# A mixture-of-experts layer behind gated linear attention: the joined passage, smaller padding, and expert numbers loaded one slot ahead

## The chip, the cores and the metric

The kernel runs on one core of a Trainium2 chip. The metric is the device time of one execution in microseconds; lower is better. The core has five engines with queues of their own: TensorE (PE in the profile, its weight loads PEld), VectorE (DVE), ScalarE (ACT), GpSimd (POOL) and SyncE (SP), which here only issues DMAs. Each engine works through its instructions in the order in which the program lists them, and semaphores order the engines against each other.

## The reference

The input is 2048 tokens of 128 channels in float32. First comes gated linear attention with 4 heads: each head carries a state through the tokens, `S = S * exp(g) + k v^T`, and the output `q S` is normalised by its RMS, gated, and projected; the layer's input is added, and a layer norm gives `x1`. Then comes the expert part:

```python
scores = x1 @ Wr + br                       # 8 experts
topk_idx = top_k(scores, 2)                 # 2 experts for each token
weights = softmax(scores over the 2 chosen)
for i in range(8):
    h = relu(x1 @ W1[i] + b1[i])            # 512 hidden
    y = h @ W2[i] + b2[i]
    out += y * weight of expert i           # for the tokens that chose i
x = layernorm(x1 + out)
```

## The kernel before, in words

The attention runs over T = 16 tiles of 128 tokens in ROUNDS = 20 software-pipelined rounds, written out by hand on every engine: in round i, tile i is scored, tile i-1 is attended (`AGE_O`), tile i-2 gets its gate (`AGE_GATE`), tile i-3 its projection, residual, layer norm and router score (`AGE_OUT`), and each pair of tiles its places among the experts' rows (`AGE_PLACE`). Two PSUM banks are handed over as wholes once in a round: PE writes bank 6 for ScalarE (`write_act_bank`) and bank 7 for VectorE (`write_dve_bank`), and it writes a bank again when the last reader is through.

The chosen rows of tokens (x1, the weight, and the number of the result row, 130 words) are scattered by POOL to a table in DRAM, `expert_rows`, in which each of the 8 experts has a region of CAP = 2176 rows (`scatter_rows`, L512 to L516; two indirect DMAs for a tile). The regions are not full, so SP first writes padding rows over all of them (L408 to L410, 8 DMAs of 1105 KB); POOL waits for the padding before the first scatter (L532).

The expert part works in SLOTS = 39 slots of 128 rows. A slot belongs to one expert; a small table in SBUF gives for every slot the expert and the first row. It is worked out on the core in two halves. The first EARLY = 13 slots follow from the first 10 tiles alone (`early_counts`, `early_pairs`, `early_positions`, `early_slots`, `early_entries`, `early_table`, a chain that alternates between PE and VectorE, begun in round EARLY_ROUND = 16); the other 26 from all tiles (`late_pairs`, `late_positions`, `late_slots`, `late_entries`, `late_table`, inside the first slots). The last of these early steps stand in round 17: PE's `early_entries` ahead of its `write_dve_bank(17)`, VectorE's `early_table` at the start of the round.

For each slot, SP reads the first row from the table and gathers 128 rows (`gather`, L419 to L433; HELD = 13 buffers, so gather 13 is the first that needs a buffer back). VectorE copies the expert's W1 out of the block of all eight (`copy_w1`, three buffers). PE then does, in one step (`pe_step(i)`), the 8 matmuls of `hidden(i + 1)` (L1425), the transpose of the rows of slot i + 2 (L1414), and the 8 matmuls of `expert_out(i)` (L1440). Of the four 128-wide chunks of a hidden layer, ScalarE does bias and ReLU of three (`hidden_lower`, L678 to L691) and VectorE of one (`hidden_upper`, L1065). ScalarE also copies the transposed rows (`copy_rows`, L671 to L676). VectorE adds the bias and weighs the result (`weighted`, L1076 to L1088), and POOL scatters it to the result table (L544). Each engine reads the expert's number with a register load (`expert_of`, L393); ScalarE does this inside `hidden_lower`, between `copy_rows(i + 1)` and the ReLUs of slot i:

```python
                e = expert_of(act, i)
                act.wait_ge(s_ha, i + 1)
                if i >= 3:
                    act.wait_ge(s_ye, i - 2)
                for n in range(LOWER):
                    act.activation(hT[:, h, n, :], bank[2 * (i % 2)][:, n * P:(n + 1) * P], ACT.Relu,
```

From FIRST_ROWS = 18 on the rounds and the slots meet, which is called the passage here. PE transposes rows 0 and 1 and runs `hidden(0)` at the end of round 18, then finishes round 19, and only then begins `pe_step(0)`. After the slots SP loads the two results of each token, and POOL, VectorE and ScalarE add them and do the last layer norm.

## Time and profile before

| what | value |
|---|---|
| time, median of 3 runs | 214.4 us (212.98, 214.9, 214.4) |
| the profiled execution's own time | 215.49 us |
| its span, first to last instruction | 213.7 us |
| mean granted TensorE clock in it | 0.921 |
| busy: PE, DVE, ACT, POOL | 176.2, 149.2, 119.9, 103.0 us |
| DMA moved | 25.72 MB |
| stages, us from the span's start | projections to 37; rounds to about 110; slots 112 to 194; end to 213.7 |

In the profile's slices of the span, PE is busy for 0.8 to 1.0 of nearly every slice from the second on, except between 101 and 112 us and after 194 us; its granted clock is 1.00 in most slices, and about a half in three stretches: 40 to 47 us, 105 to 115 us, and from 197 us on. DMA engines are busy all the time up to 59 us, and little afterwards. In the tables, a row of the timeline gives start, length, engine, line and operation, the tiles written and read, and in brackets how long the engine stood idle before it and what it waited for ("issue" where the profile shows no releaser).

### The profile page before, as it was taken

To read this page: it belongs to the slowest core of one execution; us is meant where nothing else is said; L and a number is where in the kernel's file an instruction comes from. 1 tells how busy PE (TensorE), PEld (TensorE's weight loads), DVE (VectorE), ACT (ScalarE), POOL (GpSimd) and SP (SyncE) were. 2 spreads that over 40 slices of the span, in tenths; PEclk is the share of its full clock that TensorE was granted. 3 is DMA by queue.
4 is the path that set the end of the run, shared out by engine and by line. 5 is a ranking of instruction groups with operands and counts; after the bars stand their busy time and mean duration, and the time that the engine had idled before them with its cause. 6 is when DMAs were issued, how large, how long until landed. Compare 5 with 4: busy or idle time off the path is not lost.

```text
span 213.7 us, 5544 instructions
## 1 busy us (share of the span) xinstructions
PE 176.2 (82%) x1414; PEld 141.1 (66%) x1414; DVE 149.2 (70%) x520; ACT 119.9 (56%) x382; POOL 103.0 (48%) x134
## 2 busy tenths in 40 slices
PE   2899989799797999998449999999999999992000
PEld 1546635567465777776338899999999999981000
DVE  4669993737798989888676676766766766752393
ACT  1248868444776776686246456656555555560165
POOL 6055020022526898987837745544545545544460
PEclk9999999769999999999857999999999999999555
DMA  5999999999980680111134422222222220000753
GB/s 167 278 206 211 197 200 193 205 191 155 239 258 26 139 328 33 51 35 44 37 86 105 101 66 66 73 76 56 74 74 62 70 60 21 30 9 0 246 220 123
DMA packets 33870, 25.72 MB, mean 120 GB/s; under 512 B 3310, under 2 KB 29604, under 8 KB 33840
## 3 DMA queue, kind: packets, MB, share of 16 engines
q1 hardware_dynamic: 30624, 20.96, 47.0%
q0 software_dynamic: 2272, 4.24, 5.8%
q8 instruction: 13, 0.21, 0.4%
q10 hardware_dynamic: 944, 0.17, 0.4%
q14 instruction: 17, 0.14, 0.2%
HBM read 11.03 MB, written 14.79 MB: 121 GB/s over the span
## 4 chain that ended last, share of the span: by engine, by line
PE 49%; DVE 15%; POOL 14%; issue 12%; DMA 4%; ACT 3%; ACTq 1%; DVEq 1%; POOLq 0%; SPq 0%
PE psum L1440 17%; PE psum L1425 16%; POOL expert_rows L514 7%; POOL rgate L509 4%; PE psum L1217 2%; DVE cum_and_q L807 2%; PE psum L1230 2%; POOL km L501 2%; PE psum L1414 2%; DVE v_sb L793 2%; DMA bgk_sb<-in_L_attn_bgk_dram 2%; DVE gT L802 2%; DMA gate<-expert_results 1%; DVE fstats L1178 1%; PE psum L1201 1%
## 5 line engine op out<-in xcount | busy, mean ns | idle before, releaser
L544 POOL DMA_INDIRECT expert_results<-kT,xg x39 | 38.5, 988 | 37.5 <-DVE kT L1087 33.1
L690 ACT ACTIVATE gT<-psum,b_sb 128x128 f32<-128x128 f32 x117 | 34.5, 365 | 18.1 <-issue 16.4
L1440 PE MATMUL psum<-w_sb,gT 128*128 x312 | 43.3, 282 | 1.0 <-DVE gT L1073 0.3
L1425 PE MATMUL psum<-kT,km 128*128 128x128 f32 x312 | 42.9, 282 | 0.0
L1440 PEld LDWEIGHTS psum<-w_sb,gT 128*128 128x128 f32 x312 | 37.8, 191 | 4.6 <-issue 3.7
L1425 PEld LDWEIGHTS psum<-kT,km 128*128 128x128 f32 x312 | 39.3, 198 | 0.1
L514 POOL DMA_INDIRECT expert_rows<-xr,slot x32 | 31.5, 984 | 11.2 <-issue 7.2
L1063 DVE COPY km<-cum_and_q 128x512 f32 x39 | 16.9, 433 | 16.8 <-PE psum L1425 12.8
L509 POOL TENSOR_TENSOR rgate<-rrms,gate 128x256 f32<-128x256 f32 x16 | 11.7, 734 | 30.3 <-ACT rrms L627 30.1
L676 ACT ACTIVATE kT<-psum 128x128 f32<-128x128 f32 x39 | 10.8, 277 | 16.6 <-PE psum L1414 16.6
L1081 DVE TENSOR_TENSOR kT<-psum,b_sb 128x128 f32<-128x128 f32 x39 | 11.3, 290 | 9.3 <-PE psum L1440 7.4
L1087 DVE SCALAR_TENSOR_TENSOR kT<-kT,xg 128x128 f32<-128x128 f32 x39 | 13.7, 352 | 1.5 <-DVE kT L1081 0.2
L1073 DVE TENSOR_SCALAR gT<-psum,b_sb 128x128 f32<-128x128 f32 x39 | 13.4, 345 | 0.7 <-PE psum L1425 0.5
L657 ACT ACTIVATE sq<-psum 128x256 f32<-128x256 f32 x16 | 6.1, 382 | 13.8 <-PE psum L1371 13.8
L895 DVE COPY_PREDICATED aT<-keep,psum 128x512 f32<-128x512 int32 x16 | 11.6, 724 | 1.5 <-PE psum L1271 1.5
L1414 PE MATMUL psum<-ident,xg 128*128 128x128 f32 x39 | 11.0, 281 | 1.7 <-ACT kT L676 1.7
L1303 PE MATMUL psum<-sq,block_ones 128*128 128x256 f32 x32 | 11.1, 430 | 0.7 <-ACT sq L657 0.7
L1371 PE MATMUL psum<-aT,v_sb 128*64 128x128 f32 x128 | 11.5, 303 | 0.0
L932 DVE TENSOR_TENSOR ogT<-psum,rgate 128x256 f32<-128x256 f32 x16 | 6.8, 422 | 5.3 <-POOL rgate L509 5.2
L1367 PE MATMUL psum<-qc,state 128*128 128x128 f32 x60 | 10.2, 294 | 0.0
L1334 PE MATMUL psum<-wo_sb,ogT 128*128 128x136 f32 x32 | 8.5, 350 | 1.6 <-DVE ogT L932 1.5
L490 POOL TENSOR_SCALAR x_sb<-x_sb 128x2048 f32<-128x2048 f32 x1 | 5.4, 5375 | 8.1 <-PE psum L1201 8.1
(185 smaller groups left out, 341.6 us busy)
## 6 DMA issues: line engine op xcount, KB each, us to landing
expert_rows<-pad_row SPq DMA_DIRECT2D x8, 1105.0 KB, 18.2
xg<-expert_rows SPq DMA_DIRECT2D x39, 65.0 KB
cum_and_q<-in_L_ffn_W_dram SPq DMA_DIRECT2D x8, 256.0 KB
gate<-expert_results SPq DMA_DIRECT2D x8, 256.0 KB, 4.9
x_sb<-in_L_attn_x_dram SPq DMA_DIRECT2D x4, 256.0 KB, 4.2
out_dram<-v_sb SPq DMA_DIRECT2D x8, 128.0 KB, 2.0
expert_results<-kT,xg POOLq DMA_INDIRECT x39, 2.3
b_sb<-in_L_ffn_b_dram SPq DMA_DIRECT2D x1, 512.0 KB, 16.0
```

The source lines that it names most:

```text
L509: pool.tensor_tensor(rgate[:, t % 2, :, :], rrms[:, t % 2, :, :], gate[:, :, t * P:(t + 1) * P], ALU.mult).then_inc(s_rg, 1)
L514: pool.indirect_dma_start(out=rows[:, :], in_=xr[:, t, k, :], in_offset=None, out_offset=bass.IndirectOffsetOnAxis(ap=slot[:, t, k:k + 1], ...
L544: pool.indirect_dma_start(out=results[:, :], in_=yw[:, u, :], in_offset=None, bounds_check=TOP * N - 1, oob_is_err=False, out_offset=bass. ...
L690: act.activation(hT[:, h, n, :], bank[2 * (i % 2)][:, n * P:(n + 1) * P], ACT.Relu, bias=b1_sb[:, bass.ds(e * HC + n, 1)]).then_inc(s_hTa, 1)
L895: dve.copy_predicated(aT[:, t % 2, :, :], keep[:, :].unsqueeze(1).to_broadcast([P, HEADS, P]), psum[:, 0:HEADS, 0:P]).then_inc(s_aT, 1)
L1063: dve.tensor_copy(w1_buf[i % W1S], w1_sb[:, bass.ds(e * H, H)]).then_inc(s_w1_slot, 1)
L1073: dve.tensor_scalar(hT[:, h, n, :], bank[2 * (i % 2) + 1][:, (n - LOWER) * P:(n - LOWER + 1) * P], b1_sb[:, bass.ds(e * HC + n, 1)], 0.0, ...
L1087: dve.scalar_tensor_tensor(yw[:, u, :], yb[:, h, :], xg[:, r, D:D + 1], xg[:, r, 0:D], ALU.mult, ALU.add).then_inc(s_yw, 1)
L1371: last = mm(b[r:r + dv, c * P:(c + 1) * P], v_sb[:, t, h * dv:(h + 1) * dv], aT[:, t % 2, h, :], start=(t == 0 and c == 0), stop=True, ski ...
L1414: nc.tensor.transpose(bank[5][:, 0:P], xg[:, u, 0:D], ident[:, :]).then_inc(s_gt, 1)
L1425: last = mm(bank[2 * (i % 2) + half][:, k * P:(k + 1) * P], w1_buf[u][:, n * P:(n + 1) * P], xgT[:, h, :], start=True, stop=True)
L1440: last = mm(out_bank(i)[:, 0:D], hT[:, h, n, :], w2_all[:, bass.ds(first + n * D, D)], start=(n == 0), stop=(n == HC - 1))
```

## The change

The diff does five things.

1. The padding: SP writes no longer all regions. It pads 128 rows at the end of region 0 before the rounds, and after the first 13 gathers, once VectorE has written the end of each region (`region_ends`), 128 rows behind each of them (`pad_ends`: 8 register loads and 8 DMAs). Gather 13 waits for these. POOL waits for no padding.
2. ScalarE: `load_expert(i + 1)` stands behind `hidden_lower(i)` and ahead of `copy_rows(i + 2)`.
3. The early table: VectorE's `early_slots` and `early_table` and PE's `early_entries` stand in round 16; `copy_w1(0)` in round 17, `copy_w1(1)`, `hidden_upper(0)` and `copy_w1(2)` in round 18, `hidden_upper(1)` in round 19.
4. The passage: PE transposes rows 0 at the start of round 18, and runs `pe_step(0)` in round 19 ahead of `write_dve_bank(19)`. ScalarE does `copy_rows(0)` and `(1)` at the start of round 18, `act_step(0)` and `hidden_lower(1)` at the start of round 19. The state update of the last tile, which nothing reads, is dropped on PE, ScalarE and VectorE. POOL scatters tile 10 in round 17 in place of 16.
5. The late half of the table stands a slot later on PE and VectorE.

```diff
         pad_row = sb("pad_row", [P, ROW])
+        region_end = sb("region_end", [1, E], I32)
...
         s_pad = sem("rows_padded")
+        s_ends = sem("region_ends_known")
         s_scat_early = sem("early_rows_scattered")
...
+        def carried_at(i, age):
+            t = at_age(i, age)
+            return None if t == T - 1 else t
         def batch_at(i, lag):
...
             sp.wait_ge(s_const, 4)
-            for e in range(E):
-                sp.dma_start(rows[e * CAP:(e + 1) * CAP, :].rearrange("(n p) c -> p n c", p=P),
-                             pad_row[:, :].unsqueeze(1).to_broadcast([P, CAP // P, ROW])).then_inc(s_pad, 16)
+            sp.dma_start(rows[CAP - P:CAP, :], pad_row[:, :]).then_inc(s_pad, 16)
             sp.dma_start(w2_sb[:, :, :].rearrange("p e (j d) -> p e j d", d=D),
...
                 sp.dma_start(w1_sb[:, x * H:(x + 1) * H], W1[x, :, :]).then_inc(s_w1, 16)
+            def pad_ends():
+                sp.wait_ge(s_ends, 1)
+                for e in range(E):
+                    r = sp.value_load(region_end[0:1, e:e + 1], min_val=0, max_val=E * CAP - P)
+                    sp.dma_start(rows[bass.ds(r, P), :], pad_row[:, :]).then_inc(s_pad, 16)
...
                 elif i == EARLY:
+                    sp.wait_ge(s_pad, 16 * (E + 1))
                     sp.wait_ge(s_scat_late, 16 * TOP * (T - EARLY_TILES))
...
-            for i in range(SLOTS):
+            for i in range(EARLY):
+                gather(i)
+            pad_ends()
+            for i in range(EARLY, SLOTS):
                 gather(i)
...
                     pool.wait_ge(s_xcopy, 2 * (b + 1))
-                    if b == 0:
-                        pool.wait_ge(s_pad, 16 * E)
-                    scatter_rows(2 * b)
+                    if i != T:
+                        scatter_rows(2 * b)
                 b = batch_at(i, AGE_PLACE + 2)
                 if b is not None:
+                    if i == T + 1:
+                        scatter_rows(2 * b)
                     scatter_rows(2 * b + 1)
...
-            def hidden_lower(i):
-                h = i % 3
+            lower_expert = {}
+            def load_expert(i):
                 if i == 0:
...
                     act.wait_ge(s_late_table, 2)
-                e = expert_of(act, i)
+                if i < SLOTS:
+                    lower_expert[i] = expert_of(act, i)
+            def hidden_lower(i):
+                h = i % 3
+                e = lower_expert.pop(i)
                 act.wait_ge(s_ha, i + 1)
...
             def act_step(i):
-                hidden_lower(i)
+                if i != 1:
+                    hidden_lower(i)
+                load_expert(i + 1)
                 if i + 2 < SLOTS:
...
                     act.wait_ge(s_act_bank, i + 1)
-                for age, stage in ((AGE_GATE, inverse_rms), (0, copy_kmT), (AGE_O, square_o), (AGE_OUT, inverse_std), (AGE_ROW, copy_row)):
+                if i == FIRST_ROWS:
+                    load_expert(0)
+                    copy_rows(0)
+                    copy_rows(1)
+                if i == FIRST_ROWS + 1:
+                    act_step(0)
+                    hidden_lower(1)
+                t = at_age(i, AGE_GATE)
+                if t is not None:
+                    inverse_rms(t)
+                t = carried_at(i, 0)
+                if t is not None:
+                    copy_kmT(t)
+                for age, stage in ((AGE_O, square_o), (AGE_OUT, inverse_std), (AGE_ROW, copy_row)):
                     t = at_age(i, age)
...
                     factors(groups_begun[i])
-                if i == FIRST_ROWS:
-                    copy_rows(0)
-                    copy_rows(1)
-            for i in range(SLOTS):
+            for i in range(1, SLOTS):
                 act_step(i)
...
+            def region_ends():
+                dve.tensor_tensor(region_end[:, :], bank[7][0:1, 432:432 + E], expert_row[0:1, :], ALU.add).then_inc(s_ends, 1)
             def late_pairs():
...
                     copy_w1(i + W1S)
-                if i + 1 < SLOTS:
+                if i == 0:
+                    hidden_upper(2)
+                elif 1 < i < SLOTS - 1:
                     hidden_upper(i + 1)
...
                     early_pairs()
-                if i == EARLY_ROUND + 1:
-                    early_table()
+                if i == FIRST_ROWS:
+                    copy_w1(1)
                 take(mask_scores, 0)
                 take_batch(count_hits, placing)
-                if i == EARLY_ROUND + 2:
-                    copy_w1(0)
                 if i == FIRST_ROWS + 1:
-                    copy_w1(1)
+                    dve.wait_ge(s_w2, 32)
+                    hidden_upper(1)
                 take_batch(weigh, was_placed)
...
                 take_batch(sum_places, placing)
-                take(update_state, AGE_O)
+                if i == EARLY_ROUND:
+                    early_slots()
+                if i == FIRST_ROWS:
+                    hidden_upper(0)
+                    copy_w1(2)
+                t = carried_at(i, AGE_O)
+                if t is not None:
+                    update_state(t)
                 take(gate_o, AGE_GATE)
+                if i == EARLY_ROUND:
+                    early_table()
+                if i == EARLY_ROUND + 1:
+                    copy_w1(0)
                 take(take_score, AGE_OUT)
...
                     scale_q(groups_ended[i])
-                if i == EARLY_ROUND:
-                    early_slots()
-            copy_w1(2)
-            dve.wait_ge(s_w2, 32)
-            hidden_upper(0)
             dve_step(0)
+            region_ends()
+            dve_step(1)
             late_pairs()
-            dve_step(1)
+            dve_step(2)
             late_slots()
-            dve_step(2)
+            dve_step(3)
             late_table()
-            for i in range(3, SLOTS):
+            for i in range(4, SLOTS):
                 dve_step(i)
...
-                for s, age in ((s_kmT, 0), (s_lrms, AGE_GATE)):
-                    t = at_age(i, age)
-                    if t is not None:
-                        pe.wait_ge(s, t + 1)
+                t = carried_at(i, 0)
+                if t is not None:
+                    pe.wait_ge(s_kmT, t + 1)
+                t = at_age(i, AGE_GATE)
+                if t is not None:
+                    pe.wait_ge(s_lrms, t + 1)
                 if i == 0:
...
-                for s, age in ((s_state, AGE_O), (s_res, AGE_OUT)):
-                    t = at_age(i, age)
-                    if t is not None:
-                        pe.wait_ge(s, t + 1)
+                t = carried_at(i, AGE_O)
+                if t is not None:
+                    pe.wait_ge(s_state, t + 1)
+                t = at_age(i, AGE_OUT)
+                if t is not None:
+                    pe.wait_ge(s_res, t + 1)
                 if i == 0:
...
                         centre_router()
-                    for age, stage in ((0, transpose_km), (AGE_GATE, sum_squares)):
-                        t = at_age(i, age)
-                        if t is not None:
-                            last = stage(t)
+                    t = carried_at(i, 0)
+                    if t is not None:
+                        last = transpose_km(t)
+                    t = at_age(i, AGE_GATE)
+                    if t is not None:
+                        last = sum_squares(t)
                     last.then_inc(s_act_bank, 1)
...
                     dve_bank_read(i - 1)
-                    for age, stage in ((AGE_O, update), (AGE_OUT, project_out)):
-                        t = at_age(i, age)
-                        if t is not None:
-                            last = stage(t)
+                    t = carried_at(i, AGE_O)
+                    if t is not None:
+                        last = update(t)
+                    t = at_age(i, AGE_OUT)
+                    if t is not None:
+                        last = project_out(t)
                     if i == 1:
...
                 write_act_bank(i)
-                if i == EARLY_ROUND + 1:
-                    early_entries()
+                if i == FIRST_ROWS:
+                    pe.wait_ge(s_early_table, 2)
+                    pe.wait_ge(s_og, T)
+                    transpose_rows(0)
+                if i == FIRST_ROWS + 1:
+                    pe.wait_ge(s_w2, 32)
+                    pe_step(0)
                 write_dve_bank(i)
+                if i == EARLY_ROUND:
+                    early_positions()
                 if at_age(i, AGE_O) is not None:
...
                 if i == EARLY_ROUND:
-                    early_positions()
+                    early_entries()
                 if i == FIRST_ROWS:
-                    pe.wait_ge(s_early_table, 2)
-                    transpose_rows(0)
                     transpose_rows(1)
                     hidden(0)
-            pe.wait_ge(s_w2, 32)
-            pe_step(0)
             pe_step(1)
+            pe_step(2)
             late_positions()
-            pe_step(2)
+            pe_step(3)
             late_entries()
-            for i in range(3, SLOTS):
+            for i in range(4, SLOTS):
                 pe_step(i)
 _INS = ['L0_attn_x', 'L0_attn_Wq', 'L0_attn_Wk', 'L0_attn_Wv', 'L0_attn_Wg', 'L0_attn_Wgk1', 'L0_attn_Wgk2', 'L0_attn_bgk2', 'L0_attn_Wo', 'L0_attn_g_norm_weight', 'L0_ffn_Wr', 'L0_ffn_br', 'L0_ffn_W1', 'L0_ffn_b1', 'L0_ffn_W2', 'L0_ffn_b2']

```

## Rows read from the trace of the kernel before

**Rows 1.** The head of the page.
```profile
span 213.7 us, 5544 instructions
```

**Rows 2.** Weight loads of PE in the slots, timeline: start us, us, engine line.
```profile
127.20 0.97 PEld L1440 LDWEIGHTS psum<-w_sb,gT 128*128 128x128 f32 x8
...
129.10 0.97 PEld L1440 LDWEIGHTS psum<-w_sb,gT 128*128 128x128 f32 x8
...
130.88 0.14 PEld L1414 LDWEIGHTS psum<-ident,xg 128*128 128x128 f32 x1
131.21 0.97 PEld L1440 LDWEIGHTS psum<-w_sb,gT 128*128 128x128 f32 x8 [0.19 <-issue]
```

**Rows 3.** The same of the last two slots, each cut by its window.
```profile
191.20 0.19 PEld L1440 LDWEIGHTS psum<-w_sb,gT 128*128 128x128 f32 x1 [0.17 <-issue]
...
192.49 0.30 PEld L1440 LDWEIGHTS psum<-w_sb,gT 128*128 128x128 f32 x2 [0.32 <-issue]
```

**Rows 4.** Timeline of ScalarE beside Rows 2.
```profile
129.40 0.28 ACT L676 ACTIVATE kT<-psum 128x128 f32<-128x128 f32 x1 [0.43 <-PE psum L1414]
130.20 0.88 ACT L690 ACTIVATE gT<-psum,b_sb 128x128 f32<-128x128 f32 x3 [0.52 <-issue]
```

**Rows 5.** Register loads on ScalarE's queue: duration ns min/median/max, first and last start.
```profile
L393 ACTq TENSOR_LOAD <-table x39: 273/287/393, 113.3 to 190.7; - x39
```

**Rows 6.** Timeline of VectorE: in the backlog behind the late table.
```profile
124.19 0.43 DVE L1063 COPY km<-cum_and_q 128x512 f32 x1 [0.34 <-issue]
...
125.86 0.43 DVE L1063 COPY km<-cum_and_q 128x512 f32 x1 [0.40 <-issue]
```

**Rows 7.** Timeline of PE in the passage.
```profile
104.72 0.25 PE L1465 MATMUL psum<-in_slot,pair_value 128*1 128x13 f32 x4 [2.41 <-DVE in_slot L1021]
...
109.56 0.42 PE L1414 MATMUL psum<-ident,xg 128*128 128x128 f32 x1
111.72 0.45 PE L1414 MATMUL psum<-ident,xg 128*128 128x128 f32 x1 [1.74 <-ACT kT L676]
111.96 1.93 PE L1425 MATMUL psum<-kT,km 128*128 128x128 f32 x8
...
116.21 1.15 PE L1440 MATMUL psum<-w_sb,gT 128*128 x8 [0.32 <-DVE gT L1073]
```

**Rows 8.** Granted clock of PE (third number) over the passage.
```profile
105.00:115.30 10.30, 7.07 (x41) 0.50 0.34 80
```

**Rows 9.** Timeline of VectorE in the passage.
```profile
100.72 0.18 DVE L928 BATCH_NORM_AGGREGATE mv<-stats 128x2 f32<-128x6 f32 x1
...
103.41 1.25 DVE L1021 TENSOR_SCALAR in_slot<-slot_id,pair_slot,pair_full 128x13 f32<-128x13 f32 x1
...
105.08 0.24 DVE L1028 TENSOR_SCALAR table<-psum 1x13 int32<-1x13 f32 x2 [0.17 <-PE psum L1465]
...
111.24 0.23 DVE L917 SCALAR_TENSOR_TENSOR score<-res,rstd,br_sb 128x8 f32<-128x8 f32 x1 [0.60 <-ACT rstd L653]
...
112.57 0.22 DVE L972 TENSOR_REDUCE pile<-pile 128x8 bf16<-128x40 bf16 x1
...
116.28 0.47 DVE L1063 COPY km<-cum_and_q 128x512 f32 x1 [0.32 <-issue]
...
119.64 0.43 DVE L1063 COPY km<-cum_and_q 128x512 f32 x1 [0.79 <-DVE pair_late L1036]
```

**Rows 10.** Timeline of POOL around 104 and 116 us.
```profile
103.89 0.73 POOL L509 TENSOR_TENSOR rgate<-rrms,gate 128x256 f32<-128x256 f32 x1
...
115.56 0.97 POOL L514 DMA_INDIRECT expert_rows<-xr,slot  x1 [0.57 <-issue]
```

**Rows 11.** Instructions of L514 (indirect scatters of rows): issue to landing.
```profile
DMA to landing us min/median/max: 2.3/2.4/5.7
```

**Rows 12.** SP's queue: the padding, and the first 13 gathers.
```profile
L409 SPq DMA_DIRECT2D expert_rows<-pad_row x8: 587/5570/5787, 5.7 to 36.7; - x8
...
106.31 14.04 SPq L433 DMA_DIRECT2D xg<-expert_rows  x13
```

## The prediction

> **What bounds the kernel now.** I read the slices of the page first, then PE's weight loads slot by slot, then ScalarE's and VectorE's timelines beside them, and last the passage between rounds and slots. The profiled execution took 215.49 us with a span of 213.7 [rows 1]; the median of the runs is 214.4, so 1.1 less than the execution that every duration here comes from.
>
> The slots fill some 80 us and PE is busy in all of them. That does not mean that PE alone sets their pace. From one expert_out to the next PE took 1.90 us in one case and 2.11 in the next [rows 2], and this alternation goes on: slot 6 starts at 129.10 and slot 37 at 191.20 [rows 2, 3], 62.10 us for 31 slots, a mean of 2.00. In a short slot expert_out's weights load 0.11 us behind the start of the transpose; in the long one it is 0.33 (130.88 to 131.21), and the profile names no releaser. ScalarE's rows give it: its three ReLUs started at 130.20 and took 0.88, so they ended at 131.08, and PE went on 0.13 later [rows 4]. So every second slot PE waits for ScalarE. And ScalarE is late because between copy_rows (start 129.40, 0.28 long) and the ReLUs it stood idle for 0.52 [rows 4]: that is the register load, whose first instruction alone takes 287 ns in the median, 39 times [rows 5], and what follows from it.
>
> In the passage PE waits for VectorE's in_slot for 2.41 us (until 104.72) and for ScalarE's copy for 1.74 (until 111.72) [rows 7], and its granted clock is 0.50, the lower level of 1.2 GHz, from 105.0 to 115.3 [rows 8]. The first expert_out starts at 116.21.
>
> **Part by part. ScalarE's load.** It now stands behind hidden_lower(i) and ahead of copy_rows(i + 2). ScalarE is idle there anyway: 0.43 us, waiting for PE's transpose [rows 4]. So the load costs nothing as long as PE's transpose comes later than it; if that cover were gone, copy_rows would start up to 0.45 later. After copy_rows the ReLUs can follow at once, say 0.1 after its end. The ReLUs of the long slot would then end at 129.40 + 0.28 + 0.10 + 0.88 = 130.66, and 0.13 later is 130.79, before 130.88 + 0.11 = 130.99 where PE arrives. The wait goes. ScalarE's own work in a slot, 0.28 + 0.88 + 0.1 + 0.45 = 1.7, stays below 1.90. Next in line is VectorE. Just behind the late table, when it had a backlog and waited for nobody, its copies of W1 were 1.67 apart [rows 6], also below 1.90. So PE's own 1.90 is the pace: 31 x 1.90 = 58.9 in place of 62.10, **3.2 us** less. Of the last slot (1.29 from 191.20 to 192.49 [rows 3]) I take 0.3 off for the same reason. Bounds: nothing, if another engine stops PE at the same point, and 3.5.
>
> **The early table.** In round 16 VectorE now goes to early_slots right behind mean_var (100.72 + 0.18 [rows 9]), 2.3 us before the 103.41 of today. in_slot took 1.25 us for 13 columns and ended together with POOL's multiplication (103.89 + 0.73 = 104.62 [rows 10]), so I read it as held up by POOL. In its new place it can meet the multiplication of the tile before. I give it 0.4, bounds 0.15 and 1.25. The gate of tile 14 comes next, and the table is done at about 102.5 in place of 105.32 [rows 9]. SP issues the first gather 1.0 after the table [rows 9, 12], so at 103.5. In the trace the gather landed at most 3.25 us after its issue (106.31 to 109.56, where PE takes it up directly behind other work [rows 7, 12]), while an indirect scatter of 128 rows lands after 2.3 to 5.7, median 2.4 [rows 11]. I take 2.6: rows 0 are there at 106.1.
>
> **The passage.** Up to 104.0 PE does what it does now without the 2.41 wait, then it stands for some 2 us for rows 0, with project_out(15) queued behind. I leave the clock at the lower level here. Transpose 0.4, project_out 1.5, transpose 0.4, and hidden(0) 1.73 at that clock (1.93 with the modelled end [rows 7]) bring PE to 110.3; today hidden(0) ends at 113.9 [rows 7]. VectorE meanwhile waits in round 18 for hidden(0): upper(0) at 110.35, copy_w1(2) 0.8 with its load, score to count_hits 1.55 (111.24 to 112.79 [rows 9]), upper(1) 0.35, three steps of the places 0.65, and weigh at 114.8, since ScalarE's exp_gap(7) now stands behind two sets of ReLUs (2 x 0.88). copy_w1(3) follows at 115.4, against 116.28 today [rows 9], and upper(1) is then done already, and its 0.4 too. PE starts expert_out(0) at 112.1, 4.1 us sooner than 116.21. But most of this is not kept. VectorE has the backlog: upper(2) 115.7, weighted(0) 116.1, region_ends 0.2, copy 117.4, weighted(1) 117.9, four pair steps to 119.2, copy 120.0 (the load follows these steps, 0.79 [rows 9]), upper(3) 120.35, slots 121.9, copy 122.7, upper(4) 123.05 to 123.4. PE waits at late_positions until 119.3, and starts expert_out(4) at 123.5, (5) at 125.6 and (6) at 127.5. Today (6) starts at 129.10 [rows 2]: **1.6 us** less. Bounds: nothing, if VectorE meets POOL in its moved copies, and 3.0, if hidden(0) runs at the upper clock and VectorE's chain moves up with it.
>
> **The table half, padding and small edits.** The eight padding writes took SP's queue 5.57 us each [rows 12], but POOL's first scatter did not wait for them, and W2 lands long before the slots in both orders. Their removal is worth 0 here, bounds 0 and 1, as the engines' instruction fetches share these DMA engines. The new writes have 128 rows, as a gather has. Thirteen gathers took 14.04 us of SP [rows 12], 1.14 apart; from 103.5 the last is issued by 117.5, and region_ends is done by 117. Eight more give 126.7, landed at about 129.5. Gather 13 lands at 132. PE wants its rows in step 11, at 123.5 + 7 x 1.90 = 136.8. The margin is 5 us, so it costs 0. The late table is finished near 124.3, ahead of that too. The dropped copy, transpose and update are under 0.5 us on each of three engines and lie in rounds that other chains set; POOL's gate of tile 15 no longer stands behind two scatters, 0.3 earlier. All this I count in the passage.
>
> **The sum:** 3.2 + 0.3 + 1.6 = 5.1. 215.49 - 5.1 = 210.4 for an execution like the profiled one; from the median, **209.3 us**.
>
> **A rule on POOL and VectorE.** in_slot ended with POOL's instruction [rows 9, 10], while a copy of W1 that started at 116.28, inside POOL's scatter of 115.56 to 116.53, took 0.47, hardly more than the usual 0.43 [rows 9, 10]. So a multiplication of POOL's seems to hold VectorE up and a scatter mostly not. The Trainium skill, SBUF — State Buffer, section Who interferes with whom, has it that such a VectorE copy and a POOL operation exclude each other for the whole instruction. By that rule copy_w1(0), (1) and (2), which now fall among the scatters of tiles 10 to 13, would each wait; the trace agrees for in_slot and disagrees for this copy.
>
> **Rivals, with their chances.**
> - Forecast, 0.48: own range 207.9 to 210.6.
> - The clock stays up, or comes back by 110, as PE is busy without a break from 106 on: passage 3.0 in place of 1.6, 207.9. For it: the wait of 2.41 is gone. Against: a stand of 2 us is still there. 0.13.
> - The passage gives nothing: each of three copies of W1 waits for a scatter of POOL's that is on average half over, 3 x 0.97 / 2 = 1.5 [rows 10] on VectorE's chain, which is the one that binds: 214.4 - 3.5 = 210.9. in_slot speaks for it, the copy at 116.28 against it [rows 9]. 0.16. This is what the rule above would do.
> - The load is only moved: it starts behind the last ReLU and delays copy_rows, and hidden waits for that. ScalarE's cycle is then 0.88 + 0.45 + 0.3 + 0.28 = 1.9 plus hand-overs, about 1.97; the slots gain 31 x 0.03 = 0.9: 214.4 - 0.9 - 1.6 = 211.9. Against it: the idle 0.43. 0.10. With the passage failing too, or another engine taking ScalarE's place at 2.00: 213.5, 0.08.
> - Slower: the padding writes on the path. They stand on SP ahead of gather 13. If each held SP for 5.6 us as the old ones did [rows 12], the last would be out at 117 + 8 x 6.4 = 168, 32 us after PE wants slot 13: about 245. It decides from about 1.8 us a write in place of 1.14. Against it: the old ones are 17 times as long, and 5.57 / 17 is 0.33. 0.03, and 0.02 for an unseen wait in the passage of over 7 us.
>
> The range holds the first four, 206.6 to 212.4. About 1 per cent, 2.1 us, is what a measurement tells from no change. Faster by more: 0.48 + 0.13 + 0.16 + 0.08 of the fourth = 0.85; same 0.10; slower 0.05.
>
> **What would show it.** Expert_out starts 1.89 to 1.90 apart throughout, with no ReLU ending 0.13 ahead of PE; ScalarE's load beside the ReLUs, not behind copy_rows; the table at about 102.5, first expert_out near 112, expert_out(6) near 127.5; PE held at late_positions; gather 13 landed before 136. The prediction is wrong if the slots keep a long and a short one, if VectorE's copies in rounds 17 and 18 take over 0.6, or if PE waits for rows of slot 13.

## The result

The changed kernel took 205.66 us (median of 4 runs, 204.85 to 209.29), the kernel before 214.65 beside it (4 runs, 212.98 to 219.24): a ratio of 0.959 [0.950, 0.969]. The forecast was 209.3 with a range of 206.6 to 212.4, so the direction was right and the time was missed by 3.6 us, 0.9 below the range. The ratios here and below compare the fast executions alone (3 on either side here), while the profile of before (215.49 us) and that of e4 below are of slow ones.

From the page of the changed kernel, the head, the slices of the granted clock and a DMA row:

```profile
span 204.6 us, 5566 instructions
...
PEclk9999999979999999999958999999999999998555
...
xg<-expert_rows SPq DMA_DIRECT2D x39, 65.0 KB, 1.9
```

The span is 9.1 us shorter than in [rows 1]. Where that lies is seen by cutting both spans at the same four points: the start of VectorE's masking of the last tile's attention scores (the last mask, for short), and of expert_out of slots 0, 6 and 37. The forecast's column is its own working.

| stretch, us | before | after | less | forecast |
|---|---|---|---|---|
| start to last mask | 96.0 | 93.0 | 3.0 | 0 |
| last mask to expert_out(0) | 20.2 | 14.8 | 5.4 | 4.1 |
| last mask to expert_out(6), the passage | 33.1 | 29.6 | 3.5 | 1.6 |
| 31 slots to expert_out(37) | 62.1 | 58.7 | 3.4 | 3.2 |
| expert_out(37) to the end | 22.5 | 23.4 | -0.9 | 0.3 |

Three readings follow: the slots came as forecast, the passage brought twice as much, and 3.0 us stand where nothing was forecast.

**The slots.** PE's weight loads of the changed kernel, timeline as in [rows 2], and the last two slots as in [rows 3]:

```profile
120.55 0.14 PEld L1469 LDWEIGHTS psum<-ident,xg 128*128 128x128 f32 x1
120.66 0.97 PEld L1495 LDWEIGHTS psum<-w_sb,gT 128*128 128x128 f32 x8
...
122.44 0.14 PEld L1469 LDWEIGHTS psum<-ident,xg 128*128 128x128 f32 x1
122.55 0.97 PEld L1495 LDWEIGHTS psum<-w_sb,gT 128*128 128x128 f32 x8
...
181.21 0.97 PEld L1495 LDWEIGHTS psum<-w_sb,gT 128*128 128x128 f32 x8
182.41 0.97 PEld L1495 LDWEIGHTS psum<-w_sb,gT 128*128 128x128 f32 x8 [0.23 <-issue]
```

ScalarE beside them, which answers to [rows 4], and its register loads, which answer to [rows 5]:

```profile
120.97 0.28 ACT L693 ACTIVATE kT<-psum 128x128 f32<-128x128 f32 x1 [1.03 <-PE psum L1469]
121.14 0.88 ACT L713 ACTIVATE gT<-psum,b_sb 128x128 f32<-128x128 f32 x3
```

```profile
L400 ACTq TENSOR_LOAD <-table x39: 273/279/384, 103.1 to 180.1; - x39
```

Expert_out now starts 0.11 behind every transpose, 1.89 from one to the next. The ReLUs start 0.17 behind the start of copy_rows with no idle time between them; they end at 122.02, 0.53 ahead of PE at 122.55. The load is as long as before; it only lies elsewhere.

**The passage.** PE's timeline, which answers to [rows 7]:

```profile
98.48 0.25 PE L1520 MATMUL psum<-in_slot,pair_value 128*1 128x13 f32 x4 [0.46 <-DVE in_slot L1056]
...
102.23 0.45 PE L1469 MATMUL psum<-ident,xg 128*128 128x128 f32 x1 [1.41 <-DVE ogT L967]
...
104.34 3.64 PE L1480 MATMUL psum<-kT,km 128*128 128x128 f32 x16
...
107.98 1.47 PE L1495 MATMUL psum<-w_sb,gT 128*128 x8
...
114.62 0.38 PE L1526 MATMUL psum<-pair_late,before 128*128 128x1 f32 x2 [0.67 <-DVE pair_late L1074]
```

VectorE's, which answers to [rows 9, 6]:

```profile
97.89 0.55 DVE L1056 TENSOR_SCALAR in_slot<-slot_id,pair_slot,pair_full 128x13 f32<-128x13 f32 x1
...
99.06 0.23 DVE L1063 TENSOR_SCALAR table<-psum 1x13 int32<-1x13 f32 x2
...
101.71 0.41 DVE L967 TENSOR_TENSOR ogT<-psum,rgate 128x256 f32<-128x256 f32 x1
102.46 0.43 DVE L1101 COPY km<-cum_and_q 128x512 f32 x1 [0.33 <-issue]
...
103.28 0.67 DVE L1101 COPY km<-cum_and_q 128x512 f32 x1
...
107.21 0.53 DVE L1101 COPY km<-cum_and_q 128x512 f32 x1 [0.41 <-issue]
...
110.09 0.19 DVE L1031 TENSOR_REDUCE slot<-placed 128x4 uint32<-128x32 f32 x1
110.34 0.19 DVE L1012 TENSOR_TENSOR xr<-egap,xr 128x2 f32<-128x2 f32 x1
...
119.56 0.43 DVE L1101 COPY km<-cum_and_q 128x512 f32 x1 [0.23 <-issue]
...
121.33 0.68 DVE L1101 COPY km<-cum_and_q 128x512 f32 x1 [0.49 <-PE psum L1480]
```

SP's queue, which answers to [rows 12]:

```profile
100.29 15.10 SPq L446 DMA_DIRECT2D xg<-expert_rows  x13
116.31 8.29 SPq L429 DMA_DIRECT2D expert_rows<-pad_row  x8
126.13 13.86 SPq L446 DMA_DIRECT2D xg<-expert_rows  x13
```

PE's wait for in_slot is down from 2.41 to 0.46, and the wait of 1.74 for ScalarE's copy is gone; what is left there is one of 1.41, as before had one of 1.45 (until 108.09). Its releaser is VectorE's gate of the last tile, not the rows: those had come within 1.94 of the issue at 100.29. At late_positions PE still waits for VectorE, 0.67.

**The clock.** The windows view over the two inner stretches at the lower level (columns: length; busy time and instructions of PE, PEld, DVE, ACT, POOL; granted clock; DMA share; GB/s):

```profile
40.60:44.00 3.40, 3.40 (x22) 2.18 (x22) 1.37 (x3) 1.17 (x4) 1.14 (x2) 0.50 0.03 7
...
102.00:108.80 6.80, 6.50 (x29) 6.23 (x30) 4.33 (x20) 3.92 (x18) 5.25 (x6) 0.50 0.45 106
```

In the profile of before they were 40.2 to 47.0 and 105.0 to 115.3 [rows 8]. The clock first rose at about 12.9 us there and at 9.9 here. The windows view has 1.00 from the span's start on in both, so the first rise is read from the length of equal matmuls, in before and then in the changed kernel:

```profile
10.56 1.91 PE L1217 MATMUL psum<-xT,wgk 128*128 128x512 f32 x2
```

```profile
10.03 1.02 PE L1264 MATMUL psum<-xT,wgk 128*128 128x512 f32 x2
```

The masks of the first and the third tile, in the same order, show where the 3.0 us of the start arise:

```profile
38.66 0.72 DVE L895 COPY_PREDICATED aT<-keep,psum 128x512 f32<-128x512 int32 x1
...
43.48 0.73 DVE L895 COPY_PREDICATED aT<-keep,psum 128x512 f32<-128x512 int32 x1 [0.73 <-PE psum L1271]
```

```profile
36.70 0.72 DVE L930 COPY_PREDICATED aT<-keep,psum 128x512 f32<-128x512 int32 x1
...
40.35 0.72 DVE L930 COPY_PREDICATED aT<-keep,psum 128x512 f32<-128x512 int32 x1
```

At the first tile the changed kernel is 2.0 ahead, at the third, beside the stretches that begin at 40, 3.1, and from the fourth to the last it stays 3.0 ahead.

### The profile page after: what moved, and what is told of

Its sections match the earlier page's. It is cut to its first block, busy times and chain, and to the rows that moved or that the text cites. A ratio compares the mean times of both kernels' runs of the same rounds, so it can differ in the third digit from the quotient of the medians.

```text
span 204.6 us, 5566 instructions
## 1 busy us (share of the span) xinstructions
PE 170.2 (83%) x1405; PEld 138.8 (68%) x1405; DVE 146.9 (72%) x520; ACT 115.8 (57%) x381; POOL 103.1 (50%) x134
## 3 DMA queue, kind: packets, MB, share of 16 engines
q1 hardware_dynamic: 14384, 12.51, 21.7%
## 4 chain that ended last, share of the span: by engine, by line
PE 56%; DVE 15%; issue 11%; POOL 8%; DMA 4%; ACT 3%; SPq 1%; DVEq 0%; ACTq 0%; POOLq 0%
PE psum L1480 18%; PE psum L1495 16%; DMA gate<-expert_results 3%; POOL rgate L525 2%; DVE cum_and_q L842 2%; PE psum L1469 2%; PE psum L1277 2%; PE psum L1264 2%; PE psum L1354 2%; PE psum L1422 2%; PE psum L1418 2%; DVE v_sb L828 2%; DVE gT L837 2%; POOL expert_rows L530 2%; PE psum L1248 2%
## 5 line engine op out<-in xcount | busy, mean ns | idle before, releaser
L1495 PE MATMUL psum<-w_sb,gT 128*128 x312 | 42.0, 278 | 0.2 <-issue 0.2
L1495 PEld LDWEIGHTS psum<-w_sb,gT 128*128 128x128 f32 x312 | 38.4, 194 | 0.9 <-issue 0.8
L1101 DVE COPY km<-cum_and_q 128x512 f32 x39 | 17.4, 446 | 16.5 <-PE psum L1480 13.5
L674 ACT ACTIVATE sq<-psum 128x256 f32<-128x256 f32 x16 | 6.1, 382 | 13.3 <-PE psum L1422 13.2
L1422 PE MATMUL psum<-aT,v_sb 128*64 128x128 f32 x128 | 11.0, 294 | 0.0
L1418 PE MATMUL psum<-qc,state 128*128 128x128 f32 x60 | 10.3, 296 | 0.0
L1225 DVE BATCH_NORM_STATS2 fstats<-xT 128x6 f32<-128x128 f32 x16 | 3.8, 282 | 8.3 <-POOL xT L572 8.3
L765 ACT ACTIVATE flog<-fmv,eps_sb 128x2 f32<-128x2 f32 x8 | 2.4, 296 | 12.2 <-DVE fmv L1228 12.2
```

Of the source, the lines that this page charges most:

```text
L1101: dve.tensor_copy(w1_buf[i % W1S], w1_sb[:, bass.ds(e * H, H)]).then_inc(s_w1_slot, 1)
L1418: mm(b[:, c * P:(c + 1) * P], state[:, (t - 1) % 2, c * P:(c + 1) * P], qc[:, t * P:(t + 1) * P], start=(c == 0), stop=True, skip_group_ch ...
L1422: last = mm(b[r:r + dv, c * P:(c + 1) * P], v_sb[:, t, h * dv:(h + 1) * dv], aT[:, t % 2, h, :], start=(t == 0 and c == 0), stop=True, ski ...
L1495: last = mm(out_bank(i)[:, 0:D], hT[:, h, n, :], w2_all[:, bass.ds(first + n * D, D)], start=(n == 0), stop=(n == HC - 1))
```

## The experiments

The stretches are those of the table above, in its order. Each kernel's profiled execution gives them, and the timed runs give the ratio to before, with its 95% interval. Where there was one run, its time stands in that column.

| kernel | runs | ratio to before | start to mask | to out(0) | to out(6) | 31 slots | to the end |
|---|---|---|---|---|---|---|---|
| e1 before + load ahead | 6 | 0.978 [0.967, 0.989] | 93.1 | 19.7 | 32.5 | 58.7 | 23.1 |
| e2 before + small padding | 12 | 1.001 [0.995, 1.008] | 93.0 | 20.3 | 33.5 | 62.2 | 23.5 |
| e3 after, load back | 6 | 0.986 [0.969, 1.003] | 91.9 | 14.3 | 29.8 | 61.8 | 23.4 |
| e4 after, full padding | 6 | 0.974 [0.962, 0.986] | 99.5 | 14.8 | 29.6 | 58.7 | 23.1 |
| e5 before + passage alone | 6 | 0.982 [0.967, 0.996] | 94.0 | 14.5 | 29.9 | 62.1 | 23.0 |
| e6 before + early table | 1 | 212.58 us | 93.1 | 18.8 | 32.5 | 62.2 | 23.0 |
| e7 after, late half back | 1 | 213.0 us | 100.0 | 14.1 | 29.3 | 58.7 | 23.2 |
| e8 after, again | 6 | 0.968 [0.959, 0.977] | 93.0 | 14.8 | 29.6 | 58.7 | 23.3 |
| e9 after, gather 1.0 later | 1 | 206.37 us | 92.9 | 14.9 | 29.8 | 58.7 | 23.3 |
| e10 after, step 0 back | 1 | 210.95 us | 95.0 | 18.2 | 32.8 | 58.7 | 22.7 |
| e11 after, two loads | 1 | 205.5 us | 92.4 | 15.4 | 30.1 | 58.7 | 22.6 |
| e12 after, filler on PE | 6 | 0.963 [0.955, 0.970] | 93.7 | 14.8 | 29.5 | 58.7 | 22.4 |
| e13 before, again | 1 | 216.21 us | 95.3 | 20.3 | 34.1 | 62.3 | 22.7 |
| e14 after, gather 2.1 later | 1 | 214.24 us | 100.2 | 16.3 | 31.0 | 58.7 | 22.7 |
| e15 e7 again, timed | 6 | 0.961 [0.952, 0.969] | 93.1 | 14.8 | 30.5 | 58.7 | 23.2 |

### Which part brings what (e1 to e5)

**e1, before with the load ahead.** Nothing else of the change:

```diff
             def act_step(i):
                 hidden_lower(i)
+                load_expert(i + 1)
                 if i + 2 < SLOTS:
                     copy_rows(i + 2)
...
+            load_expert(0)
             for i in range(SLOTS):
                 act_step(i)
```

> The kernel before with one edit: ScalarE reads a slot's expert one slot ahead. Theory A (every second slot of PE waits for ScalarE, whose load stands in its way): expert_out starts 1.90 us apart from slot 6 on, 3.2 to 3.8 us less than before (ratio about 0.983), and the passage is unchanged. Rival: the load is only moved and delays copy_rows instead, or VectorE takes ScalarE's place at 2.00: within 1 us of before.

The 31 slots took 58.7 us, as in the full change. The passage, expected unchanged, was 0.6 shorter (32.5); the first six slots are part of it. **e3** takes the same part out of the changed kernel (the load again inside hidden_lower):

> The changed kernel with ScalarE's load back between copy_rows and the ReLUs. Theory A: 3.2 to 3.8 us more than the changed kernel, near 209.3, with long and short slots again, so 0.976 of before. Rival: within 1 us of the changed kernel.

The 31 slots took 61.8 us. Its ScalarE and PEld timelines show the old pattern back:

```profile
127.86 0.28 ACT L693 ACTIVATE kT<-psum 128x128 f32<-128x128 f32 x1 [0.50 <-PE psum L1471]
...
128.57 0.89 ACT L715 ACTIVATE gT<-psum,b_sb 128x128 f32<-128x128 f32 x3 [0.43 <-issue]
```

```profile
127.55 0.97 PEld L1497 LDWEIGHTS psum<-w_sb,gT 128*128 128x128 f32 x8
...
129.59 0.97 PEld L1497 LDWEIGHTS psum<-w_sb,gT 128*128 128x128 f32 x8
...
131.48 0.64 PEld L1497 LDWEIGHTS psum<-w_sb,gT 128*128 128x128 f32 x5
```

A long slot of 2.04 follows one of 1.89, and the ReLUs that started at 128.57 end at 129.46, 0.13 ahead of PE at 129.59. The two sizes of the same step are 3.4 (on before) and 3.2 us (off after: 61.85 - 58.66).

**e2 and e4, the padding**, on before and off the changed kernel:

```diff
-            for e in range(E):
-                sp.dma_start(rows[e * CAP:(e + 1) * CAP, :].rearrange("(n p) c -> p n c", p=P),
-                             pad_row[:, :].unsqueeze(1).to_broadcast([P, CAP // P, ROW])).then_inc(s_pad, 16)
+            sp.dma_start(rows[CAP - P:CAP, :], pad_row[:, :]).then_inc(s_pad, 16)
...
```

The writes behind the regions (`pad_ends`) and their waits come or go with it.

> The kernel before with the small padding alone. The changed kernel was 3.0 us ahead before the passage began, which the prediction had put at 0. Theory B (the full padding's traffic up to 59 us holds something up, or shifts it): 2 to 3 us less than before (ratio about 0.988). Rival C (the lead came from the stretches in which the clock happened to be at its lower level in the one profiled execution): within 0.6 us of before, and rounds as far apart as before.

> The changed kernel with the full padding of before and without the writes behind the regions. Theory B: 2 to 3 us more than the changed kernel, near 208.3 (0.970 of before). Rival C: the same as the changed kernel within 0.6 us (0.958 of before).

With 12 runs the small padding alone shows no effect (1.001, known to 0.7 per cent, 1.5 us), and the passage and the slots of e4 are those of the changed kernel to 0.1. By its ratio of 0.974 alone e4 would be nearer to theory B (0.970) than to rival C (0.958), but the interval holds e8's 0.968 as well. The start is what needs care: e2 has 93.0 and e4 99.5, which alone would say that the padding costs 3 to 6 us. But e1, with the full padding, has 93.1, and e7 and e14, with the small one, have 100.0 and 100.2. So the length of the start goes with the execution and not with the padding. It goes with the time that the clock spent at the lower level before the last mask, from the span's start to the first rise and in the stretches after it: 10.5 us in e3 (start 91.9), 13.2 in e2 and 13.9 in e1 (93.0, 93.1), 13.3 in the changed kernel, 19.7 in before (96.0), 29.1, 30.8 and 33.3 in e4, e7 and e14 (99.5, 100.0, 100.2).

**e5, the passage alone** (parts 3 to 5 of the change on before, the old padding and load):

> The changed kernel with full padding and with ScalarE's load back: parts 3, 4 and 5 alone. From the last mask of scores to expert_out(6): 29.6 to 30.0 us in place of 33.1, slots as before (62.1 for 31), so 3.1 to 3.5 us less than before in all (ratio about 0.985). Rival (the passage needs the other two parts): 32 or more from mask to expert_out(6).

The passage went from 33.1 to 29.9, the slots stayed at 62.1: 3.2 of the passage's 3.5 us come from parts 3 to 5 by themselves. **e8** ran the changed kernel again, unedited:

> The changed kernel once more, unedited, to size what one execution's clock adds. If the 3.0 us lead before the passage was the clock's doing, fast runs are spread by 2 us or more and the ratio to before lies nearer 0.967 (7.0 us: 3.5 in the passage, 3.4 in the slots) than 0.958. If it is a property of the kernel, the ratio stays at 0.958 and the last score mask starts near 93.0 again.

Its stretches repeat to 0.1. Its ratio of 0.968 is 6.9 us, known to 2 us to either side, and passage and slots make together as much (3.5 + 3.4).

### What the passage consists of (e6, e10, e7, e15)

**e6**, only the early table's steps one round earlier, on before (VectorE's early_slots and early_table and PE's early_entries in round 16):

> The kernel before with early_slots, early_table and early_entries in round 16, nothing else. Theory P1 (the passage gained because the table is 2.9 us earlier and PE loses its 2.41 us wait): expert_out(6) starts 2 us or more sooner after the last mask than 33.1. Theory P2 (the gain is in the order of round 19 and the first slots): under 1 us sooner.

It gave 1.5 at out(0), and 0.6 at out(6) against the profile of before, 1.6 against e13, whose low stretch of the clock in the passage was longer (13.6 us):

```profile
104.10:117.70 13.60, 10.38 (x57) 9.43 (x58) 7.67 (x37) 5.64 (x24) 7.88 (x9) 0.50 0.37 85
```

That is the band within which two executions of the same kernel place out(6): 33.1 and 34.1. Against the one, the 0.6 is theory P2's, against the other it lies between the two theories; the early table alone does not bring the passage's 3.5 in either case.

> The kernel before once more, for its trace. If the segments measure the kernel and not one execution, last mask to expert_out(6) is 33.1 within 0.4 and 31 slots take 62.1 within 0.2, while the time of the last mask, 96.0 in the first trace, may lie anywhere from 92 to 100.

The slots (62.3) and the start (95.3) are as expected, the passage is not: 34.1 is 1.0 from 33.1 in place of 0.4.

**e10**, the changed kernel with step 0 again behind round 19 on PE:

```diff
-                if i == FIRST_ROWS + 1:
-                    pe.wait_ge(s_w2, 32)
-                    pe_step(0)
                 write_dve_bank(i)
...
+            pe.wait_ge(s_w2, 32)
+            pe_step(0)
             pe_step(1)
```

> The changed kernel with PE's step 0 behind write_dve_bank(19) in place of ahead of it. Theory J (joining the passage is what pays): expert_out(0) about 1.5 us later after the last mask than 14.8, expert_out(6) 1 us or more later than 29.6. Rival (the early table and the moved copies pay, the order in round 19 does not, since VectorE binds): expert_out(6) within 0.4.

Out(0) came 3.4 later and out(6) 3.2, twice or more what theory J expected. PE's timeline of e10:

```profile
106.42 1.93 PE L1480 MATMUL psum<-kT,km 128*128 128x128 f32 x8
111.08 0.20 PE L1397 MATMUL psum<-pile,before_count 128*128 128x16 bf16 x2 [2.73 <-issue]
...
111.40 2.05 PE L1480 MATMUL psum<-kT,km 128*128 128x128 f32 x8
```

PE waits 2.73 us behind hidden(0) for the last tile's hits (the profile names no releaser; VectorE's row of the hits ends at 110.98); in the changed kernel hidden(1) fills that hole (the row of 16 matmuls at 104.34). Joining round and step is the mechanism of the passage: without it the rest of the change brought 0.3 us against the profile of before and 1.3 against e13. Part of the 3.2 is the clock's: the low stretch in the passage lasted 10.2 us here (104.1 to 114.3) in place of 6.8, and hidden(1) took 2.05 where a hidden at the upper level takes 1.1. The two go together in all profiles: with step 0 ahead of the bank (the changed kernel, e3, e4, e5, e7, e8, e9, e11, e12, e14, e15) that stretch lasted 3.4 or 6.8 us, without it (before, e1, e2, e6, e10, e13) 10.2 or 13.6. How the 3.2 divides between hole and clock was not tried.

**e7 and e15**, the late half of the table back where it stood:

```diff
             dve_step(0)
             region_ends()
+            late_pairs()
             dve_step(1)
-            late_pairs()
+            late_slots()
             dve_step(2)
-            late_slots()
-            dve_step(3)
             late_table()
...
```

> The changed kernel with the late half of the table where it stood before. If moving it pays, expert_out(6) comes 0.5 us or more later after the last mask than the 29.6 of the changed kernel, as PE waits longer at late_positions; if VectorE's backlog alone binds, the steps only change places and it stays within 0.3.

> The changed kernel with the late half of the table where it stood before, timed. One trace had expert_out(6) at 29.3 after the last mask in place of 29.6, with a shorter stretch at the lower clock. If the late half is better left where it was, fast runs take 0.3 us less than the changed kernel's (ratio to before 0.966 in place of 0.968) and the segment is 29.3 again at a like clock; if it was the clock, 29.6 or more. Either is below what the ratio can tell; the segment decides.

The two profiles disagree: out(6) is 0.3 sooner than in the changed kernel in e7 and 0.9 later in e15 (29.3 and 30.5 against 29.6). The clock is a likely reason: e7's low stretch in the passage was 3.4 us long, e15's 6.8, as long as in the changed kernel, though it began 10.3 us after the last mask there and 9.1 in the changed kernel. By the expectation's own rule (29.6 or more at a like clock) the half is not better left where it was; what moving it is worth is not shown, and the ratios cannot tell it (0.961 against 0.968 and 0.959). In e15 PE waits 1.49 at late_positions in place of 0.67:

```profile
113.68 0.38 PE L1525 MATMUL psum<-pair_late,before 128*128 128x1 f32 x2 [1.49 <-DVE pair_late L1074]
```

### The rows, the load and the clock (e9, e14, e11, e12)

**e9 and e14** put two and four register loads of SP ahead of gather 0:

```diff
                 if i == 0:
                     sp.wait_ge(s_scat_early, 16 * TOP * EARLY_TILES)
+                    for _ in range(2):
+                        sp.value_load(table[0:1, 1, 0:1], min_val=0, max_val=E * CAP - P)
```

> The changed kernel with two more register loads on SP ahead of the first gather, about 1.0 us. The prediction took 2.6 us for a gather's landing where the changed kernel shows 1.9. Theory G (rows 0 arriving later passes straight through to the slots): expert_out(6) starts 0.6 to 1.0 us later after the last mask than 29.6. Rival: PE waited there for VectorE's ogT, not for the rows, and VectorE's backlog swallows it: within 0.3.

> The changed kernel with four more register loads on SP ahead of the first gather, about 2.1 us. The same edit at 1.0 us moved expert_out(6) by 0.2, in an execution whose clock came back 3.4 us sooner. Theory G (rows 0 are on the path): expert_out(0) 1.5 to 2 us and expert_out(6) 1.2 us or more later than 14.8 and 29.6. Rival (VectorE's backlog hides it): expert_out(6) within 0.5.

Rows 0 in PE's timeline, e9 and then e14:

```profile
103.25 0.30 PE L1471 MATMUL psum<-ident,xg 128*128 128x128 f32 x1 [2.49 <-DMA xg<-expert_rows]
...
105.05 2.85 PE L1482 MATMUL psum<-kT,km 128*128 128x128 f32 x16
```

```profile
111.99 0.45 PE L1471 MATMUL psum<-ident,xg 128*128 128x128 f32 x1 [3.94 <-DMA xg<-expert_rows]
```

And SP's first issue in e9:

```profile
101.34 1.46 SPq L448 DMA_DIRECT2D xg<-expert_rows  x2
```

In e9 the rows are what PE waits for, and they come 1.91 after the issue. In e14 the landing took 2.3 (111.99 against an issue at 109.72). Against the last mask they are 10.4 in e9 (103.25 - 92.89), 11.8 in e14 (111.99 - 100.18) and 9.3 in the changed kernel. e14 ends the passage 1.4 later at 2.5 us of delay. e9 with 1.1 ends it 0.2 later, but its low stretch of the clock lasted 3.4 us in place of 6.8, and its 16 matmuls of hidden took 2.85 in place of 3.64, which gives back 0.8. So delay of the rows goes into the passage at something over a half; an exact share is not to be had from one profile each.

**e11**, ScalarE's load done twice in every slot:

```diff
                 if i < SLOTS:
+                    expert_of(act, i)
                     lower_expert[i] = expert_of(act, i)
```

> The changed kernel with ScalarE's load done twice, 0.45 us more a slot at the same place. The prediction had ScalarE at 1.7 of 1.9 us with one load and put the load behind the ReLUs. Theory S (the load runs on the queue while the ReLUs still run, so it costs ScalarE nothing): 31 slots still take 58.7 us. Rival (it stands in line): a cycle of 2.15 in place of 1.90, 66.6 us for 31 slots.

```profile
L400 ACTq TENSOR_LOAD <-table x78: 271/280/451, 102.5 to 180.6; - x78
```

78 loads, and the 31 slots still took 58.7: in its new place the load lies wholly beside the ReLUs and the wait for the transpose, and there is room for another. The passage was 0.5 longer (30.1), which one profile does not tell from chance.

**e12**, 14, 8 and 12 matmuls on constants in three holes of PE, to bring the clock up and keep it there:

```diff
+            def keep_busy(n, b=0):
+                for _ in range(n):
+                    mm(bank[b][:, P:2 * P], ones_count[:, :], ones_count[:, :], start=True, stop=True)
...
+                    keep_busy(12)
```

> The changed kernel with matmuls of constants, whose results nobody reads, in three holes of PE: 14 before the first transpose, 8 in round 0, 12 at the start of round 18. Theory K (what is left between executions is the clock's lower level after these holes): the stretches at 1.2 GHz at 40 us and in the passage shrink or go, the clock rises sooner in the first stage, fast runs take 1.5 to 3 us less than the changed kernel's (ratio to before 0.957) and spread less. Rival: the clock does as before and the fillers cost up to 1 us (ratio 0.972).

The clock first rose at 12.9, not sooner. At 40 us there was no stretch and that in the passage was 3.4 us long, but another stood at 67.5, and the windows of e12 show it at the lower level with PE at work the whole time:

```profile
105.10:108.50 3.40, 3.40 (x17) 3.40 (x17) 0.96 (x4) 1.75 (x7) 2.71 (x3) 0.50 0.45 118
67.50:70.90 3.40, 3.40 (x24) 2.62 (x24) 2.60 (x10) 2.11 (x9) 2.90 (x5) 0.50 0.59 193
```

Its ratio of 0.963 [0.955, 0.970] is between the two of the changed kernel, and out(6) came at 29.5, as without the fillers. No version beat the changed kernel beyond its interval.

## Why the prediction was off

**ScalarE's load: right.** Forecast 3.2, measured 3.4 in the full change, 3.4 in e1 and 3.2 in e3. The pace of 1.90, PE as the bound behind it and the cover of the load are all as written. The rival in which the load is only moved is refuted by e11. Of the last slot 0.09 came of 0.3 (1.29 to 1.20).

**The early table: right.** Forecast 6.5 us after the last mask (102.5 on the clock of before), seen 6.3; the first gather at 7.3 against 7.5. in_slot took 0.55 for the 0.4 taken, and it ended with POOL's multiplication again (97.89 + 0.55 = 98.44 against 97.68 + 0.72 = 98.40).

**The passage: the mechanism right, the size not.** This is one of the two steps that failed: 1.6 forecast, 3.5 measured, and also beyond its bound of 3.0. e10 shows the mechanism, and the gap of 1.9 can be followed along the forecast's own chain, in us after the last mask:

| point | forecast | after | gap gained here |
|---|---|---|---|
| PE takes rows 0 | 10.1 | 9.3 | 0.8 |
| VectorE's weigh | 18.8 | 17.4 | 0.6 |
| PE passes late_positions | 23.3 | 21.7 | 0.2 |
| expert_out(6) | 31.5 | 29.6 | 0.3 |

The first term is the landing of the gather, taken as 2.6 from [rows 11], an indirect scatter, and from one bound of 3.25; it was 1.91 in e9 and at most 1.94 here, and 0.2 are the earlier table. Little more was to be had there: the wait that ended last was not that for the rows, as forecast, but that for VectorE's gate, which ends 9.2 after the last mask. The second is exp_gap, ScalarE's exponentials for the tokens' weights: I let weigh wait for ScalarE behind two sets of ReLUs, but it began at 110.34, when VectorE's own last step of the places ended at 110.28, with no idle time, and ScalarE had been done at 110.31. The bound of 3.0 was set by the clock alone and so took in neither term. The second profile of the changed kernel (e8) has the same four times, to 0.1; e9 and e14 support the first term by experiment, the second was not tried alone. VectorE stayed the engine that binds late_positions, as forecast. The rival in which the clock comes back by 110, 14.0 after the last mask, came in part: the low stretch ended 15.9 after it (108.8), against 19.3 in before. The forecast had left the clock low and did not connect its length with the joined step.

**The start: 3.0 us that no part of the sum had.** The sum was made against one profiled execution, and it took the start as equal in both, without a reason given. It is not, from one execution to the next: over the profiles of this case it runs from 91.9 to 100.2, in kernels that are alike there, and it was 96.0 before and 93.0 after. e1, e2, e4, e7 and e14 show that it goes with no edit, and it grows with the time at the lower clock. In the profiled pair most of the 2.0 at the first tile stands behind the sooner first rise (of it, 0.4 stood before it: the matmuls of L1217 and L1264 began at 8.00 and 7.62), and the other 1.1 behind the shorter stretch at 40. The tail moved the other way, by 0.9, also without an edit that touches it (22.4 to 23.5 over the other profiles). This is the other step that failed: the term was put at nothing, and the range had no room for where the clock's low stretches fall. With 3.5 in place of 1.6 for the passage the same sum gives 207.4, which is inside the range; the 1.7 us from there to 205.66 are of this kind. The 6 runs of e8 give 0.968, 207.5 us on the 214.4 of the forecast, inside the range; the 4 runs of the result give 205.66. The changed kernel itself took 206.41 at a mean granted clock of 0.933 and 204.85 at 0.946. I take 6.9 us as what the edits are worth, because it is also the sum of the two stretches they touch; how much of the 2 us beyond it in the first comparison is chance, the intervals leave open.

**Padding: right, as far as the runs can tell.** Zero forecast, 1.001 [0.995, 1.008] measured. The eight new writes took 8.29 us of SP, and the second set of gathers went out from 126.13; PE waited for no row in the slots. The rival with the writes on the path is refuted.

**The rival in which VectorE's copies wait for POOL** did not come. POOL's timeline of the changed kernel, scatters beside the copies of W1 (L1101) in VectorE's above:

```profile
102.77 0.95 POOL L530 DMA_INDIRECT expert_rows<-xr,slot  x1 [0.30 <-ACT xr L660]
...
106.56 0.96 POOL L530 DMA_INDIRECT expert_rows<-xr,slot  x1 [0.30 <-issue]
...
119.48 0.98 POOL L561 DMA_INDIRECT expert_results<-kT,xg  x1 [0.30 <-DVE kT L1125]
120.77 0.98 POOL L561 DMA_INDIRECT expert_results<-kT,xg  x1 [0.30 <-issue]
```

The three moved copies took 0.43, 0.67 and 0.53 where an undisturbed one takes 0.43: 0.34 in all, not 1.5. The 0.67 is over the 0.6 that the prediction had named as a sign against it, but it cost 0.24. The same three took 0.43, 0.64 and 0.43 in before, and the second of them speaks against the prediction's reading that a scatter mostly does not hold VectorE up:

```profile
113.31 0.64 DVE L1063 COPY km<-cum_and_q 128x512 f32 x1 [0.52 <-issue]
```

The two longer ones started 0.51 and 0.65 into a scatter, and both ended 0.22 to 0.23 behind its end (103.95 against 103.72, 107.74 against 107.52); so did the copy at 116.28 in [rows 9, 10] (116.75 against 116.53), and one in the slots ended 0.26 behind (121.33 + 0.68 against 121.75). The copy at 119.56, 0.08 into a scatter, took its 0.43 and was through before the scatter was. So it is the last part of a scatter that holds a copy up, and none of these lost more than 0.25 to it. In e8 it went the other way: a copy that began 0.51 into a scatter took its 0.43, and the scatter took 1.05 in place of 0.96. The Trainium skill, SBUF — State Buffer, section Who interferes with whom, has such a copy and a POOL operation exclude each other; the trace agrees for the last part of a scatter and disagrees for the part before it.

## What to carry to other kernels

A register load between two dependent instructions holds its engine up for 0.4 to 0.5 us each time, even if the engine looks half idle; here some 0.2 of that reached PE in every second slot, 3.4 us of 62. One slot ahead, beside work already under way, it cost the slots nothing. Where two pipelines meet, look for what the one has waiting while the other stands idle at a hand-over, and place the ready work there: here one step of 16 matmuls in a hole of 2.7 us, with the shorter low stretch of the clock that went with it, was nearly the whole gain of the passage. Before a sum is trusted to a microsecond, cut two executions of the same kernel at the same points: the stretches that differ without an edit are the width of the range, and a short ratio of few runs carries them along.

## What was not expected of the hardware

- The granted clock's stretches at the lower level move between executions of one kernel: the changed kernel had 40.6 to 44.0 in one profile and 54.2 to 57.6 in another, e12 67.5 to 70.9, and before's low stretch in the passage was 10.2 and 13.6 us long. Matmuls on constants did not prevent them (e12). The time at the lower level before the last mask, 10.5 to 33.3 us, moved the start from 91.9 to 100.2.
- In the passage the joined step and a shorter low stretch came together in all 17 profiles: 3.4 or 6.8 us with it, 10.2 or 13.6 without.
- A gather of 128 rows lands in 1.9 us at the median, an indirect scatter of as many in 2.4 [rows 11]; the one was no measure for the other.
- SP spends 1.0 to 1.2 us on each DMA of 128 rows with an address from a register, in either direction: 13 gathers in 15.10 us, 8 padding writes in 8.29.
